# Attention with a learned metric and a small MLP on one core: setup and first block reordered, slots counted on

## The chip, the cores and the metric

One Trainium2 chip, one NeuronCore. The metric is the device time of one execution in microseconds, as the median of several runs. The engines are called TensorE (PE in the rows), VectorE (DVE), ScalarE (ACT), GpSimd (POOL) and SyncE (SP); SP's and POOL's queues issue the DMAs.

## The reference

The input x has 2048 tokens of 128 dimensions; there are 16 heads of 8 dimensions.

```python
h = layernorm(x) * (1 + ca) + sa
# attention
y = project(h)                                   # clip to +-8, y0 = sqrt(1 + sum(y^2) + eps)
v = d * dirv / (dn + eps)                        # log map: d = arccosh(y0), three square roots and a log
q, k, vv = v @ Wq.T, v @ Wk.T, v @ Wv.T
g = tanh(tanh((h - mu) @ W1.T + b1) @ W2.T + b2) * 0.1 + eta      # the metric, absolute value by sign
sc = (q * g) @ k.T / sqrt(8)                     # per head, 2048 x 2048
out = softmax(sc) @ vv
x = x + ga * project(mu0 + 0.1 * out @ Wo.T)
# MLP, 384 hidden, int weights scaled by 1/127
h = layernorm(x) * (1 + cb) + sb
x = x + gb * ((silu(h @ wg.T) * (h @ wu.T)) @ wd.T)
```

sa, ca, ga, sb, cb, gb are vectors from one small product.

## The kernel before

**Shapes.** Queries and keys are tiled in four blocks of 512 tokens (NB = 4), heads in four groups of four (NG = 4), keys in 16 tiles of 128. A query block is 64 steps: step j is head group j // 16 and key tile j % 16. In a step TensorE computes the scores of four heads in two halves (`score`, L703, 8 matmuls each, every one 32 columns wide, into one slot of two PSUM banks), ScalarE takes the exponential of each half (L510, 128x1024), and TensorE multiplies the exponentials of two steps earlier with the values (`product`, L720), accumulated over a head group in bank 6. VectorE evacuates bank 6 at each end of a head group (`evacuate`, L1100, `o_evac`); the first product of the next group waits for it.

**Slots.** There are three score slots, banks 0 to 5; half u of a block uses slot u % 3, so each block starts with slot 0, although 128 halves don't divide by 3. The exponentials lie in a ring of three steps, with an exception at the last step (`ring`). In steps 1 and 63 the product goes ahead of the first scores (`early`).

**Precision.** Queries and keys are split in three bf16 parts (hi, mid, lo), stored to DRAM and loaded back head by head with copies (SP's queue; POOL's queue for later blocks): `K_op`, `Q_op`. An extra row of the scores carries minus a bound on them: the square root of (largest key norm x query norm), per head and query. `nk` and `nq` are the norm products, `k_max` the reduction, `bound` the square root (ScalarE, L473), `shift` the scaled result (VectorE, L1013), which SP loads into `Q_op`.

**Setup.** Layer norm; transposes of h (L560) and copies (L420, `copy_hT`) for all blocks; the first metric product (`metric1`, L572); VectorE's chain for the log map with square roots and a logarithm from ScalarE (L435, L448); tanh of the metric; transposes of the values (`v_T`, `copy_vT`); keys (`k_of`, L609), the second metric product (`metric2`, L585), queries of block 0 (`q_of`). Keys of the blocks take turns in banks 2 and 3, the four norm products take turns in bank 0. Then a few idle matmuls (`keep_warm`, L674), the waits, and the loop. Each engine's queue runs in the order written.

**Work inside the loop.** In block 0 (`later`): value products (`v_of`, `V_AT`) behind steps 0, 1, 3 and 5, evacuated by VectorE (`values`, L1031); metric, queries and norms of blocks 1 to 3 at the steps of `M1_AT`, `M2_AT`, `Q_AT`, `NQ_AT`, all in bank 7 (`M_bank`); the three later roots by ScalarE behind step 49 (`ROOT_AT`). VectorE copies the norms out of bank 7 (`queries_norm`, L1065, gives `nq_sb`), and the next block's first metric product waits for that:

```python
if m == 0:
    pe.wait_ge(*((S["v_done"], NB) if b == 1 else (S["nq_sb"], b - 1)))
```

In blocks 1 to 3 the tail of the block before runs at the steps of `AT_...`: output projection, transposes, three gate and three up products (8 matmuls of 512 columns each) with a tanh each on ScalarE (L527), and four parts of the down product. All of them use bank 7. The last block's tail follows the loop. A second pass (p = 1) is there for scores beyond the bound; its branch is not taken here.

## Time and profile before

| | us |
|---|---|
| median of 3 runs | 607.02 (606.62 to 607.74) |
| profiled execution | 608.64 |
| span of its instructions | 606.6 |
| TensorE busy | 544.9 |
| ScalarE busy | 524.8 |
| VectorE busy | 152.6 |

Times in the rows are microseconds from the span's start, unless a column is said to be ns. A row of the timeline merges equal instructions that follow each other (x is how many), and what stands in brackets is the engine's idle time before it and what ended it. PEclk is the clock granted to TensorE, as a share of its full speed.

### The profile page before, as it was taken

To read this page: it belongs to the slowest core of one execution; us is meant where nothing else is said; L and a number is where in the kernel's file an instruction comes from. 1 tells how busy PE (TensorE), PEld (TensorE's weight loads), DVE (VectorE), ACT (ScalarE), POOL (GpSimd) and SP (SyncE) were. 2 spreads that over 40 slices of the span, in tenths; PEclk is the share of its full clock that TensorE was granted. 3 is DMA by queue.
4 is the path that set the end of the run, shared out by engine and by line. 5 is a ranking of instruction groups with operands and counts; after the bars stand their busy time and mean duration, and the time that the engine had idled before them with its cause. 6 is when DMAs were issued, how large, how long until landed. Compare 5 with 4: busy or idle time off the path is not lost.

```text
span 606.6 us, 16308 instructions
## 1 busy us (share of the span) xinstructions
PE 544.9 (90%) x7196; PEld 239.8 (40%) x7196; DVE 152.6 (25%) x420; ACT 524.8 (87%) x595; POOL 21.5 (4%) x25
## 2 busy tenths in 40 slices
PE   1466998999979999999999999999999999999544
PEld 0232543554423334455323444554334444543122
DVE  6963303030310361100003611000016211000363
ACT  3564898999999999999999999999999999999401
POOL 2300100000000010000000100000001000000010
PEclk9576999999989999999999999999999999999958
DMA  6012267010030200001002100000000000010000
GB/s 186 3 37 84 91 164 183 3 35 3 28 106 1 70 22 10 3 11 37 10 3 53 37 11 1 11 27 20 2 10 2 11 1 11 2 45 1 1 0 23
DMA packets 13626, 20.64 MB, mean 34 GB/s; under 512 B 2027, under 2 KB 10347, under 8 KB 13267
## 3 DMA queue, kind: packets, MB, share of 16 engines
q1 hardware_dynamic: 12707, 17.22, 11.0%
q0 software_dynamic: 560, 1.97, 0.9%
q8 instruction: 58, 0.95, 0.7%
q10 hardware_dynamic: 288, 0.40, 0.2%
q14 instruction: 13, 0.11, 0.1%
HBM read 13.15 MB, written 4.19 MB: 29 GB/s over the span
## 4 chain that ended last, share of the span: by engine, by line
PE 64%; ACT 15%; DVE 7%; issue 7%; DMA 4%; SPq 1%; POOL 0%; ACTq 0%; DVEq 0%
PE ps L703 27%; PE ps L720 26%; ACT probs L510 13%; PE ps L639 8%; DMA K_op<-k_scr 2%; DVE probs L939 1%; DMA k_scr<-arena 1%; DMA probs<-x_dram 1%; PE ps L674 1%; PE ps L609 1%; DVE arena L1143 1%; ACT arena L440 1%; SPq L262 0%; DVE kmax L1008 0%; PE ps L735 0%
## 5 line engine op out<-in xcount | busy, mean ns | idle before, releaser
L510 ACT ACTIVATE probs<-ps 128x1024 f32<-128x1024 f32 x512 | 481.4, 1116 | 16.9 <-PE ps L703 15.3
L703 PE MATMUL ps<-Q_op,K_op 73*32 73x512 bf16 x4096 | 293.0, 381 | 10.7 <-ACT probs L510 6.7
L720 PE MATMUL ps<-probs,V_op 128*32 128x512 f32 x2048 | 273.1, 595 | 1.2 <-ACT probs L510 0.8
L703 PEld LDWEIGHTS ps<-Q_op,K_op 73*32 73x32 bf16 x4096 | 122.5, 96 | 232.7 <-issue 120.5
L720 PEld LDWEIGHTS ps<-probs,V_op 128*32 128x32 f32 x2048 | 71.3, 110 | 49.3 <-issue 5.4
L1100 DVE COPY O_sb<-ps 128x512 f32<-128x512 f32 x16 | 11.1, 692 | 154.4 <-PE ps L720 154.4
L560 PE MATMUL ps<-fixed_sb,arena 128*128 128x128 f32 x32 | 7.4, 391 | 15.1 <-POOL arena L384 11.1
L1203 DVE SCALAR_TENSOR_TENSOR arena<-arena,ps 128x512 f32<-128x512 f32 x12 | 8.3, 688 | 45.0 <-ACT arena L527 45.0
L522 ACT ACTIVATE arena<-ps 128x512 f32<-128x512 f32 x4 | 2.8, 705 | 18.5 <-PE ps L735 18.5
L1209 DVE TENSOR_TENSOR arena<-ps,arena 128x512 f32<-128x512 f32 x12 | 8.3, 692 | 40.4 <-PE ps L639 40.3
L378 POOL TENSOR_TENSOR small<-small,half 128x4 f32<-128x4 f32 x4 | 4.1, 1014 | 404.6 <-DVE small L1173 404.6
L1221 DVE TENSOR_TENSOR arena<-ps,mod 128x512 f32<-128x512 f32 x3 | 2.1, 692 | 59.9 <-PE ps L639 59.9
L985 DVE TENSOR_SCALAR arena<-arena,cols 128x512 f32<-128x512 f32 x4 | 1.9, 485 | 60.2 <-ACT arena L431 60.2
L639 PE MATMUL ps<-w_att_sb,arena 128*32 128x128 f32 x256 | 10.2, 309 | 5.7 <-DVE arena L1147 5.7
L674 PE MATMUL ps<-ones_bf 128*128 128x512 bf16 x16 | 7.3, 627 | 7.9 <-POOL small L378 7.9
L1143 DVE RECIPROCAL arena<-arena 128x512 f32<-128x512 f32 x4 | 13.4, 3352 | 0.1
L639 PE MATMUL ps<-wd_f,arena 128*32 128x128 f32 x384 | 13.2, 272 | 0.0
L639 PE MATMUL ps<-arena,wg_f 128*32 128x512 f32 x96 | 12.9, 601 | 0.0
L560 PEld LDWEIGHTS ps<-fixed_sb,arena 128*128 128x128 f32 x32 | 5.3, 198 | 18.9 <-issue 8.4
L639 PE MATMUL ps<-arena,wu_f 128*32 128x512 f32 x96 | 12.7, 592 | 0.0
L639 PE MATMUL ps<-Q_op,w_sb 128*32 128x512 f32 x96 | 12.5, 591 | 0.0
L639 PEld LDWEIGHTS ps<-wd_f,arena 128*32 128x32 f32 x384 | 11.6, 109 | 2.3 <-issue 0.6
(162 smaller groups left out, 241.6 us busy)
## 6 DMA issues: line engine op xcount, KB each, us to landing
...
```

The costliest lines, as they stand in the source:

```text
L440: act.activation(h_tm[:, t, :], x_tm[:, t, :], ACT.Identity, scale=rstd[:, t:t + 1], bias=nmr[:, t:t + 1]).then_inc(S["xn_done"], 1)
L510: act.activation(probs[:, 2 * ring(j) + half_, :], slot_bank(u % 3), ACT.Exp)\
L560: ins = pe.transpose(bank(b % 2)[:, P * t:P * (t + 1)], src[:, TPB * b + t, :], ident_sb)
L609: pe.matmul(bank(2 + b % 2), wk_sb, vT[:, b, :], start=True, stop=True).then_inc(S["k_ps"], 1)
L639: ins = pe.matmul(to[CW * c:CW * (c + 1), :], weights[:, CW * c:CW * (c + 1)], moving, start=start, stop=stop, tile_position=(0, CW * c))
L674: ins = pe.matmul(to, ones_bf[:, 0:P], ones_bf[:, 0:BT], start=True, stop=True)
L703: ins = pe.matmul(slot_bank(u % 3)[CW * c:CW * (c + 1), i, :], K_op[0:rows, kt // TPB, h, at_k:at_k + CW], Q_op[0:rows, at_q:at_q + BT], s ...
L720: ins = pe.matmul(O_bank[32 * i:32 * (i + 1), :], V_op[:, kt, VW * h:VW * h + 32], probs[:, 2 * ring(j) + i // 2, BT * (i % 2):BT * (i % 2 ...
L1100: dve.tensor_copy(O_sb[:, g, :], O_bank).then_inc(S["o_evac"], 1)
L1143: c.did(dve.reciprocal(rec_T, rec_T))
L1203: dve.scalar_tensor_tensor(gl[m], th[m], 1.0, gates, ALU.add, ALU.mult).then_inc(S["gated"], 1)
L1209: dve.tensor_tensor(hid[:, m, :], ups, gl[m], ALU.mult).then_inc(S["glu_done"], 1)
```

## The change

- All four value products and their evacuations stand ahead of the loop, in banks 1 and 7 by turns; the loop waits for the last of them.
- The first block's metric (both products, three tanh) stands beside the normalisation, ahead of the roots of the log map; ten idle matmuls follow it. ScalarE loads the table of the square root once more right behind the logarithm.
- Each key block has its own bank (2 to 5); the key norms go to four groups of 32 rows of bank 0, with one reduction over all and three short copies. The key splits of blocks 1 to 3 come later in VectorE's order.
- The square roots for the query blocks 1 to 3 are computed on VectorE: a first guess by a shift and an addition on the bits, then one step with a reciprocal. `nq_sb` comes with the last operation; `shift(b)` follows at once, ahead of `evacuate(0, 2)` for the last block.
- In the first pass slots and ring are numbered on over all blocks, and no step is an exception; ScalarE's loop over blocks is written out.
- The tail's places in blocks 1 to 3 are spread over steps 8 to 55, and VectorE's evacuations of groups 1 and 2 are moved ahead of the last gate and of the result.

```diff
-AT_WO, AT_TR, AT_GATE, AT_UP, AT_DOWN = 8, 15, (19, 24, 29), (22, 27, 32), (37, 39, 41, 43)
-V_AT = (0, 1, 3, 5)
-M1_AT, M2_AT, Q_AT, NQ_AT, ROOT_AT = ((7, 10), (21, 24), (35, 38)), (13, 27, 41), (16, 30, 44), (19, 33, 47), 49
+AT_WO, AT_TR, AT_GATE, AT_UP, AT_DOWN = 8, 15, (19, 27, 35), (23, 31, 39), (43, 47, 51, 55)
+M1_AT, M2_AT, Q_AT, NQ_AT = ((7, 10), (21, 24), (35, 38)), (13, 27, 41), (16, 30, 44), (19, 33, 47)
...
-shift_f = [O_sb[0:H, 0, :], O_sb[0:H, 3, :], x_res[0:H, :, :].rearrange("p a b -> p (a b)"),
-           h_tm[0:H, 0:TPB, :].rearrange("p a b -> p (a b)")]
+shift_f = [O_sb[0:H, 0, :]] + [O_sb[0:H, 3, :]] * (NB - 1)
+root_a = x_res[0:H, :, :].rearrange("p a b -> p (a b)")
+root_b = sp_tm[0:H, 0:TPB, :].rearrange("p a b -> p (a b)")
...
-def ring(j):
-    return j % RING if j < STEPS - 1 else 1
+def slot(Bk, p, u):
+    return (u + 2 * STEPS * Bk) % 3 if p == 0 else u % 3
+def early(p, j):
+    return p == 1 and j in (1, STEPS - 1)
+def ring(Bk, p, j):
+    if p == 0:
+        return (STEPS * Bk + j) % RING
+    return 1 if j == STEPS - 1 else j % RING
...
+    pool.memset(hs_bf[:, H:2 * H], 0.0).then_inc(S["zero_ready"], 1)
...
-    for b in range(NB):
-        copy_hT(b)
+    copy_hT(0)
+    for m in range(MH):
+        tanh1(0, m)
+    copy_hT(1)
+    tanh2(0)
+    copy_hT(2)
+    copy_hT(3)
     root(y0, a2, 2)
     root(rt, t2, 3)
     root(dn, inn, 4)
     act.wait_ge(S["ln_in"], 1)
     act.activation(ln_u, u, ACT.Ln).then_inc(S["ln_out"], 1)
+    act.wait_ge(S["const_ready"], 2)
+    act.activation(kmax[:, 7:8], half[:, 0:1], ACT.Sqrt)
...
-    def k_split1(b):
+    def k_square(b):
+        act.wait_ge(S["k_ps"], b + 1)
+        act.activation(sqks[b], bank(2 + b), ACT.Square).then_inc(S["k_sq"], 1)
+    def k_high(b):
         act.wait_ge(S["k_ps"], b + 1)
         if b == 3:
             act.wait_ge(k_st[0], 16 * PARTS)
-        act.activation(k_parts[b][:, 0, :], bank(2 + b % 2), ACT.Identity).then_inc(S["k_hi"], 1)
-        act.activation(sqks[b], bank(2 + b % 2), ACT.Square).then_inc(S["k_sq"], 1)
+        act.activation(k_parts[b][:, 0, :], bank(2 + b), ACT.Identity).then_inc(S["k_hi"], 1)
...
-    def bound(b):
-        act.activation(shift_f[b], bank(6)[0:H, :] if b == 0 else shift_f[b], ACT.Sqrt,
+    def bound():
+        act.wait_ge(S["nq_ps"], 1)
+        act.wait_ge(S["kmax_ready"], 1)
+        act.activation(shift_f[0], bank(6)[0:H, :], ACT.Sqrt,
                        scale=kmax[0:H, NB:NB + 1]).then_inc(S["bound"], 1)
...
-    for m in range(MH):
-        tanh1(0, m)
     copy_vT(0)
     copy_vT(1)
-    k_split1(0)
-    tanh2(0)
+    k_square(0)
+    k_high(0)
+    copy_vT(2)
+    k_square(1)
+    q_split1()
     act.wait_ge(S["k_res"], 1)
     act.activation(k_parts[0][:, 1, :], rks[0], ACT.Identity).then_inc(S["k_mid"], 1)
-    q_split1()
-    k_split1(1)
+    k_square(2)
     act.wait_ge(S["q_res"], 1)
     act.activation(q_parts[0][:, 1, :], rqs[0], ACT.Identity).then_inc(S["q_mid"], 1)
-    k_split1(2)
-    k_split1(3)
     act.activation(sqq[:, :], g_fm[:, 0, :], ACT.Square).then_inc(S["q_sq"], 1)
-    bound(0)
+    k_square(3)
+    k_high(1)
+    bound()
     act.activation(silu_c[:, 1:2], c_c, ACT.Exp).then_inc(S["exp_table"], 1)
+    k_high(2)
+    k_high(3)
...
-            if j == ROOT_AT:
-                bound(b)
-    def block_steps(Bk, tails):
+    def block_steps(Bk, tails, p):
-                act.activation(probs[:, 2 * ring(j) + half_, :], slot_bank(u % 3), ACT.Exp)\
+                act.activation(probs[:, 2 * ring(Bk, p, j) + half_, :], slot_bank(slot(Bk, p, u)), ACT.Exp)\
...
     def blocks(p):
-        block_steps(NB * p, False)
-        with act.Fori(NB * p + 1, NB * (p + 1)) as Bk:
-            block_steps(Bk, True)
+        block_steps(NB * p, False, p)
+        if p == 0:
+            for Bk in range(1, NB):
+                block_steps(Bk, True, p)
+        else:
+            with act.Fori(NB * p + 1, NB * (p + 1)) as Bk:
+                block_steps(Bk, True, p)
...
-    for b in range(NB):
-        metric_T(b)
+    metric_T(0)
     for m in range(MH):
         metric1(0, m)
+    metric_T(1)
+    metric2(0)
+    metric_T(2)
+    metric_T(3)
...
     def k_of(b):
-        pe.wait_ge(*((S["vT_sb"], b + 1) if b < 2 else (S["vT_late"], b - 1)))
+        pe.wait_ge(*((S["vT_sb"], b + 1) if b < 3 else (S["vT_late"], 1)))
+        pe.wait_ge(S["m1_sb"], MH)
+        pe.matmul(bank(2 + b), wk_sb, vT[:, b, :], start=True, stop=True).then_inc(S["k_ps"], 1)
+    def v_of(b):
         if b >= 2:
-            pe.wait_ge(S["k_sq"], b - 1)
-            pe.wait_ge(S["k_res"], b - 1)
+            pe.wait_ge(S["v_done"], b - 1)
         else:
-            pe.wait_ge(S["m1_sb"], MH)
-        pe.matmul(bank(2 + b % 2), wk_sb, vT[:, b, :], start=True, stop=True).then_inc(S["k_ps"], 1)
-    def v_of(b):
-        pe.wait_ge(*((S["v_done"], b) if b else (S["q_f"], 1)))
+            pe.wait_ge(*((S["q_f"], 1) if b else (S["vT_late"], 1)))
         for t in range(TPB):
-            ins = by_columns(M_bank[:, P * t:P * (t + 1)], vT[:, b, P * t:P * (t + 1)], wv_sb)
+            ins = by_columns((M_bank if b % 2 else bank(1))[:, P * t:P * (t + 1)],
+                             vT[:, b, P * t:P * (t + 1)], wv_sb)
         ins.then_inc(S["v_ps"], 1)
     def nk(b):
         pe.wait_ge(S["k_sq"], b + 1)
-        pe.wait_ge(*((S["nk_done"], b) if b else (S["vT_late"], 1)))
-        pe.matmul(bank(0)[0:H, :], hs_bf[:, :], sqks[b], start=True, stop=True).then_inc(S["nk_ps"], 1)
+        pe.wait_ge(S["vT_sb"], 3)
+        pe.matmul(bank(0)[2 * H * b:2 * H * (b + 1), :], hs_bf[:, :], sqks[b], start=True, stop=True,
+                  tile_position=(0, 2 * H * b)).then_inc(S["nk_ps"], 1)
...
+    keep_warm(10, bank(5))
     v_T(0)
     v_T(1)
     k_of(0)
-    metric2(0)
+    q_of(0)
     v_T(2)
+    k_of(1)
     v_T(3)
-    q_of(0)
-    for b in range(1, NB):
-        k_of(b)
+    k_of(2)
     pe.wait_ge(S["hs_ready"], 1)
+    pe.wait_ge(S["zero_ready"], 1)
+    nk(0)
+    k_of(3)
+    nk(1)
+    nk(2)
+    nq(0)
+    nk(3)
     for b in range(NB):
-        nk(b)
-    nq(0)
+        v_of(b)
-        if j in V_AT:
-            v_of(V_AT.index(j))
...
-        if u >= 3:
+        if u >= 3 or (p == 0 and not start):
             pe.wait_ge(S["exped"], Bk * 2 * STEPS + u - 2)
         elif u < 2 and not start:
             pe.wait_ge(S["exped"], Bk * 2 * STEPS + u - 1)
...
-            early = j in (1, STEPS - 1)
-            if not early:
+            if not early(p, j):
                 score(Bk, j, p, 0)
             if j >= 2:
-                product(Bk, j - 2)
+                product(Bk, p, j - 2)
             elif tails:
-                product(Bk - 1, STEPS + j - 2)
-            if early:
+                product(Bk - 1, p, STEPS + j - 2)
+            if early(p, j):
                 score(Bk, j, p, 0)
...
-    keep_warm(7, M_bank)
-    for done, n in (("vT_late", 2), ("k_sq", NB), ("k_res", NB), ("nk_done", NB), ("bound", 1)):
+    pe.wait_ge(S["v_done"], NB)
+    keep_warm(4, M_bank)
+    for done, n in (("vT_late", 1), ("k_sq", NB), ("k_hi", NB), ("k_res", NB), ("nk_done", 1), ("bound", 1)):
         pe.wait_ge(S[done], n)
     blocks(0)
...
     dve.tensor_scalar(a2, n2, 1.0, EPS, ALU.add, ALU.add).then_inc(S["root_in"], 1)
+    def metric(b):
+        vec.after()
+        dve.wait_ge(S["m2_sb"], b + 1)
+        vec.did(dve.tensor_scalar(g_fm[:, b, :], g_fm[:, b, :], 0.1 * DH ** -0.5, eta_s, ALU.mult, ALU.add))
+    metric(0)
     dve.wait_ge(S["root_out"], 2)
...
-    def k_max(b):
-        dve.wait_ge(S["nk_ps"], b + 1)
-        dve.tensor_reduce(kmax[0:H, b:b + 1], bank(0)[0:H, :], AX.X, ALU.max).then_inc(S["nk_done"], 1)
+    def k_max():
+        dve.wait_ge(S["nk_ps"], NB)
+        dve.tensor_reduce(kmax[:, 0:1], bank(0), AX.X, ALU.max).then_inc(S["nk_done"], 1)
+        dve.wait_ge(S["nk_done"], 1)
+        for b in range(1, NB):
+            vec.did(dve.tensor_copy(kmax[0:H, b:b + 1], kmax[2 * H * b:2 * H * b + H, 0:1]))
+        vec.after()
+        dve.tensor_reduce(kmax[0:H, NB:NB + 1], kmax[0:H, 0:NB], AX.X, ALU.max).then_inc(S["kmax_ready"], 1)
     def shift(b):
-        dve.wait_ge(S["bound"], b + 1)
+        dve.wait_ge(*((S["nq_sb"], b) if b else (S["bound"], 1)))
         dve.tensor_scalar(shift_bf[b], shift_f[b], -1.0 - 2.0 ** -7, HEADROOM, ALU.mult, ALU.add)\
             .then_inc(S["shift_ready"], 1)
     def k_rest(b):
-        dve.wait_ge(S["k_sq"], b + 1)
-        dve.tensor_tensor(rks[b], bank(2 + b % 2), k_parts[b][:, 0, :], ALU.subtract)\
+        dve.wait_ge(S["k_hi"], b + 1)
+        dve.tensor_tensor(rks[b], bank(2 + b), k_parts[b][:, 0, :], ALU.subtract)\
             .then_inc(S["k_res"], 1)
...
     def queries_norm(b):
         dve.wait_ge(S["nq_ps"], b + 1)
-        dve.tensor_copy(shift_f[b], M_bank[0:H, :]).then_inc(S["nq_sb"], 1)
+        vec.did(dve.tensor_scalar(root_a, M_bank[0:H, :], kmax[0:H, NB:NB + 1], None, ALU.mult))
+        vec.after()
+        vec.did(dve.tensor_scalar(root_b.bitcast(I32), root_a.bitcast(I32), 1, None,
+                                  ALU.logical_shift_right))
+        vec.after()
+        vec.did(dve.tensor_scalar(root_b.bitcast(I32), root_b.bitcast(I32), 0x1FBD0000, None,
+                                  ALU.add))
+        vec.after()
+        vec.did(dve.reciprocal(shift_f[b], root_b))
+        vec.after()
+        vec.did(dve.tensor_tensor(shift_f[b], shift_f[b], root_a, ALU.mult))
+        vec.after()
+        vec.did(dve.tensor_tensor(root_b, shift_f[b], root_b, ALU.add))
+        vec.after()
+        dve.tensor_scalar(shift_f[b], root_b, 0.5, None, ALU.mult).then_inc(S["nq_sb"], 1)
+    copy_vT(3)
+    queries(0)
     k_rest(0)
-    copy_vT(2)
-    copy_vT(3)
-    metric(0)
+    queries_rest(0)
     k_low(0)
-    queries(0)
-    queries_rest(0)
-    k_rest(1)
     queries_low(0)
-    k_rest(2)
-    k_max(0)
-    k_max(1)
-    k_rest(3)
-    k_max(2)
-    k_max(3)
-    dve.wait_ge(S["nk_done"], NB)
-    dve.tensor_reduce(kmax[0:H, NB:NB + 1], kmax[0:H, 0:NB], AX.X, ALU.max).then_inc(S["kmax_ready"], 1)
-    k_middle(1)
-    k_low(1)
-    shift(0)
+    k_max()
     dve.wait_ge(S["ones_ready"], 1)
     values(0)
+    shift(0)
     values(1)
+    k_rest(1)
+    k_middle(1)
+    values(2)
+    k_low(1)
+    values(3)
+    k_rest(2)
+    k_rest(3)
     k_middle(2)
     k_low(2)
-    values(2)
     k_middle(3)
     k_low(3)
-    values(3)
...
         queries_norm(b)
+        shift(b)
     evacuate(0, 2)
-    for b in range(1, NB):
-        shift(b)
...
             for m in range(NM):
+                if m == NM - 1:
+                    evacuate(Bk, 1)
                 tail.gated(m, M_bank)
                 tail.glu(m, M_bank)
-            evacuate(Bk, 1)
+            evacuate(Bk, 2)
             tail.result()
-            evacuate(Bk, 2)
```

## Rows read from the trace of the kernel before

**Rows 1.** The page: busy times, the chain that ended last.

```profile
PE 544.9 (90%) x7196; PEld 239.8 (40%) x7196; DVE 152.6 (25%) x420; ACT 524.8 (87%) x595; POOL 21.5 (4%) x25
...
PE 64%; ACT 15%; DVE 7%; issue 7%; DMA 4%; SPq 1%; POOL 0%; ACTq 0%; DVEq 0%
```

**Rows 2.** Timeline of ScalarE in the loop (start, duration, instruction, count, idle).

```profile
188.58 8.53 ACT L510 ACTIVATE probs<-ps 128x1024 f32<-128x1024 f32 x9
...
198.66 1.94 ACT L510 ACTIVATE probs<-ps 128x1024 f32<-128x1024 f32 x2 [0.27 <-PE ps L703]
...
233.87 0.85 ACT L527 ACTIVATE arena<-ps 128x512 f32<-128x512 f32 x1
234.34 9.74 ACT L510 ACTIVATE probs<-ps 128x1024 f32<-128x1024 f32 x10
...
283.78 36.77 ACT L510 ACTIVATE probs<-ps 128x1024 f32<-128x1024 f32 x40 [0.27 <-PE ps L703]
...
289.23 19.41 ACT L510 ACTIVATE probs<-ps 128x1024 f32<-128x1024 f32 x21
...
307.31 1.33 ACT L510 ACTIVATE probs<-ps 128x1024 f32<-128x1024 f32 x1
```

**Rows 3.** The chain that ended last, between 212 and 222 us (start, us, what).

```profile
213.90 0.86 PE ps L703 x16
...
220.81 0.86 PE ps L703 x16
```

**Rows 4.** Timeline of the setup.

```profile
25.84 2.94 PE L572 MATMUL ps<-Q_op,w_sb 128*128 128x512 f32 x4
...
27.26 0.21 ACT L435 ACTIVATE small<-small 128x16 f32<-128x16 f32 x1 [0.49 <-DVE small L944]
...
57.70 1.05 PE L703 MATMUL ps<-Q_op,K_op 73*32 73x512 bf16 x16 [2.24 <-DMA Q_op<-wmod_sb]
```

**Rows 5.** Three windows (busy us of each engine, then PEclk, DMA share, GB/s).

```profile
20.00:24.50 4.50, 1.46 (x6) 0.72 (x4) 4.43 (x13) 1.37 (x2) 2.25 (x2) 0.50 0.00 0
...
92.80:96.20 3.40, 2.08 (x28) 0.81 (x32) 0.46 (x1) 2.48 (x4) 0.00 (x0) 1.00 0.80 187
171.40:174.70 3.30, 3.29 (x24) 0.98 (x28) 0.00 (x0) 2.71 (x3) 0.00 (x0) 0.50 0.63 159
```

**Rows 6.** Timeline of the first block's steps 0 to 17.

```profile
58.36 1.94 ACT L510 ACTIVATE probs<-ps 128x1024 f32<-128x1024 f32 x2 [1.91 <-PE ps L703]
...
67.43 0.89 DVE L1031 COPY V_op<-ps 128x128 f32<-128x128 f32 x4 [2.38 <-PE ps L639]
...
76.48 1.02 ACT L510 ACTIVATE probs<-ps 128x1024 f32<-128x1024 f32 x1 [0.16 <-PE ps L703]
...
94.12 0.61 PE L703 MATMUL ps<-Q_op,K_op 73*32 73x512 bf16 x8 [1.74 <-DMA K_op<-k_scr]
```

**Rows 7.** Timeline around the later roots.

```profile
164.87 1.28 ACT L473 ACT_TABLE_LOAD   x1
...
170.49 0.61 PE L703 MATMUL ps<-Q_op,K_op 73*32 73x512 bf16 x8 [3.71 <-ACT probs L510]
```

**Rows 8.** Timeline around the query norms of the second and the fourth block.

```profile
102.71 0.68 DVE L1065 COPY O_sb<-ps 16x512 f32<-16x512 f32 x1 [1.33 <-PE ps L634]
...
105.78 1.21 PE L639 MATMUL ps<-Q_op,w_sb 128*32 128x512 f32 x8
...
160.08 0.68 DVE L1065 COPY arena<-ps 16x512 f32<-16x512 f32 x1 [1.52 <-PE ps L634]
...
163.99 1.07 PE L720 MATMUL ps<-probs,V_op 128*32 128x512 f32 x8
```

**Rows 9.** One row of the page, then two of the timeline: VectorE's operations.

```profile
L1143 DVE RECIPROCAL arena<-arena 128x512 f32<-128x512 f32 x4 | 13.4, 3352 | 0.1
...
99.50 0.69 DVE L997 TENSOR_TENSOR arena<-arena 128x512 f32<-128x512 f32 x1
...
168.48 0.34 DVE L1117 TENSOR_SCALAR wg_f<-wg_f 128x384 f32<-128x384 int32 x1
```

More of the change, by code:

```diff
@@ L107, in build @@
         place_num, place_den = fixed_sb[:, P + H:P + H + 32], fixed_sb[:, P + H + 32:P + H + 64]
-        hs_bf = sb("hs_bf", [P, H], BF16)
+        hs_bf = sb("hs_bf", [P, 2 * H], BF16)
         silu_c = sb("silu_c", [P, 2])
@@ L633, in nq @@
                 pe.wait_ge(S["q_f"], b + 1)
-                pe.matmul((M_bank if b else bank(6))[0:H, :], hs_bf[:, :], sqq[:, :], start=True, stop=True)\
+                pe.matmul((M_bank if b else bank(6))[0:H, :], hs_bf[:, 0:H], sqq[:, :], start=True, stop=True)\
                     .then_inc(S["nq_ps"], 1)
@@ L641, in by_columns, with keep_warm @@
                 return ins
+            def keep_warm(n, to):
+                for _ in range(n):
+                    ins = pe.matmul(to, ones_bf[:, 0:P], ones_bf[:, 0:BT], start=True, stop=True)
+                ins.then_inc(S["warm"], 1)
+            keep_warm(10, bank(5))
             v_T(0)
@@ L669, in later @@
                         nq(b)
-            def keep_warm(n, to):
-                for _ in range(n):
-                    ins = pe.matmul(to, ones_bf[:, 0:P], ones_bf[:, 0:BT], start=True, stop=True)
-                ins.then_inc(S["warm"], 1)
             def score(Bk, j, p, half_):
@@ L710, in score, with product @@
                 ins.then_inc(S["scores"], 1)
-            def product(Bk, j):
+            def product(Bk, p, j):
                 g, kt = divmod(j, NT)
@@ L801, in blocks @@
                         block_steps(Bk, True, p)
-                product(last, STEPS - 2)
-                product(last, STEPS - 1)
+                product(last, p, STEPS - 2)
+                product(last, p, STEPS - 1)
                 pe.wait_ge(S["o_evac"], NG * (last + 1))
@@ L882, in _ @@
             vec.did(dve.memset(flag_f[:, :], 1.0))
+            dve.wait_ge(S["c_in"], 16)
+            vec.did(dve.tensor_scalar(eta_s, eta_c, DH ** -0.5, None, ALU.mult))
             for b in range(NB):
@@ L979, in _ @@
                 ins.then_inc(S["v_ready"], 1)
-            def metric(b):
-                vec.after()
-                dve.wait_ge(S["m2_sb"], b + 1)
-                vec.did(dve.tensor_scalar(g_fm[:, b, :], g_fm[:, b, :], 0.1 * DH ** -0.5, eta_s, ALU.mult, ALU.add))
             def queries(b):
@@ L1032, in values @@
                         V_op[:, TPB * b + t, 0:H * VW].rearrange("p (h w) -> p h w", h=H)[:, :, 0:DH],
-                        M_bank[:, P * t:P * (t + 1)].rearrange("p (h i) -> p h i", h=H))
+                        (M_bank if b % 2 else bank(1))[:, P * t:P * (t + 1)].rearrange("p (h i) -> p h i", h=H))
                     if t < TPB - 1:
```

16 lines of the change are left out of this document (5 added, 11 removed).

## The prediction

> **What bounds the kernel now.** I read the page first: TensorE is busy 544.9 us and ScalarE 524.8 us of 606.6, and the chain that ended last runs mostly over TensorE, with ScalarE second [rows 1]. Two engines that close are a pipeline, so I went to the order of time. The reader is to see three stretches: the setup up to the first scores at 57.70 [rows 4], four query blocks of 64 steps, and the last block's tail. In the loop ScalarE sets a floor: 20 exponentials start between 289.23 and 307.31, 0.904 us apart, so a step (two of them) takes 1.808 us [rows 2]. TensorE without side work needs less: its step pieces start at 213.90 and, four steps later, at 220.81, so 1.727 [rows 3]. It recovers 0.081 us a step of whatever it lost. Everything above 1.808 per step is therefore either side work that TensorE can't recover, ScalarE work that is no exponential, or a wait. I priced the change as sums over this floor.
>
> **Setup.** Rows 4 hold its two ends: the square root that the logarithm of the values starts from is asked of ScalarE and served at 27.26, and the first scores start at 57.70. The new order puts the first metric ahead of that root on ScalarE's queue, in strict order: copy, two tanh, copy, tanh, two copies, then a table load. TensorE's first metric product starts when the first copy is done, near 20.0. Its four passes took 2.94 us with the clock rising half way [rows 4]; it showed 0.50 between 20 and 24.5 [rows 5], where I take 3.6, so 23.6, tanh to 24.3, second product 1.9 at the full clock to 26.4 (3.6 at the lower one, to 28.1), tanh to 27.1, transposes and two copies to 28.3, table load 1.28 [rows 7] to 29.6. The root is 2.4 us late, and the values with it; VectorE has its own metric step done by then, so that costs nothing. In exchange the tanh work no longer stands between the values and the keys, and the four key norms no longer take turns with four reductions in one bank. By adding the same operations in the new order I get: first key product done 38.7, first query 42.6, last key norm 46.7, one reduction and three short copies to 48.0, square root of the first bound (no table load ahead of it) 48.8. Then VectorE has four value evacuations of 0.89 [rows 6], the first shift of 0.41, and, among others, three key remainders of 0.69 [rows 9], and TensorE waits for the last value block and the last remainder: 55.5. The query load, three issues behind the split of the queries, and the shift behind it land at about 55.6. First scores 55.7 against 57.70; with the ramp of the first exponential **1.7 us won**. If the second metric product runs at the lower clock, nothing is won (28.1 for 26.4, and all behind it 1.7 later); if the loads or the remainders are a little quicker, 3. Bounds: +1.5 and -3.5.
>
> **Values out of the loop.** The first 16 exponentials start between 58.36 and 76.48: 18.12 us, where 16 x 0.904 is 14.46 [rows 2, 6]. The 3.66 over the floor are the four value products of 32 matmuls and the lower clock of the start. Afterwards 0.5 stays for the ramp: **3.1 won**. It is hidden before the loop behind VectorE's chain, which is in the 55.7 above already.
>
> **The key load.** At 94.12 TensorE waits 1.74 us for the load of the second head group [rows 6]. By adding its operations in the new order, VectorE has split the last key block some 8 us behind the first shift; before, the four value evacuations wait between the splits for products in the loop (one of them at 67.43 [rows 6]). So the stores on POOL's queue and the loads behind them on SP's queue leave some 10 us earlier. The wait goes: **1.7 won**.
>
> **The later roots.** Before, ScalarE does three of them with a table load on either side: the load starts at 164.87, where the next exponential was due (164.6), and the next exponential starts at 169.42, 4.8 us late. TensorE, 3.71 us without work [rows 7], then shows clock 0.50 in the next stretch [rows 5], and ScalarE waits another 0.9 to 1.0 for it. Taken away: **5.8 won**. The table load is 1.283 us with the square root right behind it. "ScalarE: Activation LUTs" of the Trainium skill, section What ACT_TABLE_LOAD costs, counts a drain with each switch, about 2.66 us in all; two switches would then be 5.3 and the stop about 7.4. The trace measured 4.8, so the sum stays with it.
>
> What VectorE does instead: seven operations on 16x512 in a chain, each waiting for the one before, and only the last gives the semaphore that the old copy gave. Multiply from PSUM 0.68 (like the copy that it replaces [rows 8]); shift and add on integers, 0.34 for 384 columns [rows 9], so 0.43 each; reciprocal 3.35 [rows 9] (it has 128 partitions there, but the copies on 16 and on 128 partitions cost the same 0.68 to 0.69, so it is the 512 columns that count); two two-input operations at 0.69 [rows 9]; a last multiply of 0.41; six gaps of 0.04. Sum 6.9 us, against 0.68.
>
> Who waits: the next block's first metric product reads the same bank, and asks for this semaphore. Before, the copy starts at 102.71 and the product is reached at 105.78, so 3.07 us are free [rows 8]; the chain ends at +6.9, so TensorE stops 3.85 us. The same for the third block, with 3.25 free: 3.65. TensorE's queue is in order, the next scores stand behind it, and ScalarE has only 0.2 us of scores in hand there. Loss 3.7 + 3.4.
> The third chain starts at 160.08 and has no product behind it, but VectorE's own queue has: the shift (0.41) and then the evacuation of the third head group (0.69), which the first product of the fourth group waits for. It ends at 160.08 + 6.9 + 0.04 + 0.41 + 0.04 + 0.69 = 168.2; the product was reached at about 163.6 and started at 163.99 [rows 8]. Behind it stands the second half of the scores of this step: the second exponential of it starts at 169.6 and not at 165.5. Loss 4.1. So the stop of ScalarE turns into three of TensorE: **11.2 lost**.
> The clock: a wait of 1.74 left it at 1.00 [rows 5, 6], one of 3.71 sent it to 0.50 [rows 5, 7]. The new ones are 3.85, 3.65 and 4.6. At 0.50 TensorE's step is near 3.45 us, and with nothing in hand the stretch loses up to 1.6; the old case lost 1.0. I take 1.1 for the third and 0.75 x 1.6 for each of the others, where the stop may fall less well: **3.5 lost**; bounds 0 and 5. "TensorE: Matmul & The Clock Gate" of the Trainium skill, section HAM oscillation, says the same against this change: waits between bursts of matmuls make each burst start at the low clock. Rows 7 and 5 agree for 3.71 us.
>
> **Slots counted on.** Between 188.58 and 198.66, over the block's end, ten exponentials take 10.08 us and not 9.04 [rows 2]: the slots start over at 0 and TensorE waits for one still being read. With running numbers this goes, 1.04 at each of three ends, 0.5 at the last: **3.6 won** (at least 2, if VectorE's evacuation is late next).
>
> **The later tail places.** Behind the first gate's tanh, 49 exponentials start between 234.34 and 283.78: 49.4 us, floor 44.3 and two tanh of 0.47 (233.87 to 234.34) [rows 2]: 4.2 over it, TensorE being the bound throughout. The work stays the same; spread over 12 more steps it can use 12 x 0.081 = 1.0 more of ScalarE's pace. I take 0.9 in each of three blocks: **2.7 won** (bounds 0 and 4). VectorE's two reordered evacuations lie 10 steps before what needs them. ScalarE's unrolled loop I cost at nothing: blocks 0 and 1 already show the same 0.904.
>
> **Sum.** -1.7 - 3.1 - 1.7 - 5.8 + 11.2 + 3.5 - 3.6 - 2.7 = -3.9. The span of 606.6 becomes 602.7; the profiled execution took 608.64 with it, the median of the runs is 607.02, 0.4 above the span, so I forecast **603.1**.
>
> **The rivals.** (a) The forecast, three stops with the lower clock behind them: 603.1; chance 0.5, own range 601 to 605.5. (b) The stops are there, the clock stays, and the setup wins 3: 603.1 - 3.5 - 1.3 = 598.3, to 601; 0.2. For it: the new stops may straddle two stretches; against it [rows 5, 7]. (c) The change's roots don't stop anybody, because the reciprocal is short on 16 partitions (the price of 16 columns, 0.25, is no guide): chain 4.2, free time 3.07, stops of 1.1, 0.9 and 1.4 in place of 11.2, no clock: 603.1 - 7.8 - 3.5 = 591.8; 0.05. (d) The other side: VectorE's chain is longer than its parts. Only the integer operations are shown with another shape and other ALU functions; each extra us counts three times, since every stop has no cover left. From 1.7 us more per chain (8.6 in all) the gain is gone; with both integer operations at the reciprocal's 3.35 it would be 5.8 more, 17 us, 620. A milder form, 2.4 more a chain: 610. Chance 0.15. (e) The setup is not won, the metric at the lower clock: 603.1 + 1.7 to 3.2 = 605 to 606.3; 0.1.
> Below 597.5 lies (c) and a little of (b), above 609 half of (d): range 597.5 to 609. A change of 0.2% is 1.2 us here, about what a measurement of this kernel tells from none. Faster (under 605.8): (a), (b), (c) and half of (e), 0.80 less 0.06 for the upper edge of (a): 0.74; same 0.11 (the rest of (e) and that edge); slower 0.15, which is (d).
>
> **What would show it.** Right: scores start near 55.7; TensorE waits of 3 to 4.6 us for the root chain's last operation at two metric products, and for an O_sb copy at the start of the fourth head group; clock 0.50 behind them; no table load inside the loop; no gaps of 0.27 at block ends. Wrong: a reciprocal of 16x512 far from 3.35, the root of the logarithm later than 31, first scores later than 58, or block ends that still wait.

## The result and the profile after

The changed kernel takes 610.15 us (median of 9 runs, 609.16 to 611.84), the kernel before 607.74 on the same chips (9 runs, 604.7 to 609.02): ratio 1.0043, 95% interval 1.0024 to 1.0061. It is slower, by 0.4%. The forecast was 603.1, faster, with a range of 597.5 to 609, and the result lies outside it. The profiled execution took 609.74 with a span of 607.9 (before: 608.64 and 606.6). Times and ratios are those of fast runs; of one kernel of the experiments (evac_first) two of ten runs, 971.57 and 2000.25 us, are left out by this.

The page of the changed kernel: busy times, chain, and the group of the exponentials (busy us, mean ns | idle before, releaser).

```profile
PE 545.7 (90%) x7203; PEld 240.7 (40%) x7203; DVE 167.8 (28%) x437; ACT 519.4 (85%) x593; POOL 21.6 (4%) x26
...
PE 83%; DVE 8%; ACT 4%; DMA 2%; issue 1%; SPq 1%; POOL 0%; DVEq 0%
...
L528 ACT ACTIVATE probs<-ps 128x1024 f32<-128x1024 f32 x512 | 478.6, 1123 | 30.9 <-PE ps L732 29.4
```

Beside [rows 1] TensorE's busy time is the same, ScalarE's is 5.4 less (no tables and roots in the loop), and the span is no shorter: the exponentials now stand idle for 30.9 us before they start. The chain holds 83% TensorE instead of 64%.

The start of the changed kernel, timeline of TensorE and ScalarE: metric, root, first scores, first exponentials.

```profile
19.95 3.78 PE L594 MATMUL ps<-Q_op,w_sb 128*128 128x512 f32 x4 [1.58 <-ACT Q_op L431]
...
24.51 2.35 PE L607 MATMUL ps<-Q_op,w_sb 128*128 128x512 f32 x4
...
30.06 0.22 ACT L446 ACTIVATE small<-small 128x16 f32<-128x16 f32 x1
...
56.34 4.46 PE L732 MATMUL ps<-Q_op,K_op 73*32 73x512 bf16 x40 [1.59 <-DMA Q_op<-wmod_sb]
...
57.42 4.69 ACT L528 ACTIVATE probs<-ps 128x1024 f32<-128x1024 f32 x5 [5.84 <-PE ps L732]
63.21 12.24 ACT L528 ACTIVATE probs<-ps 128x1024 f32<-128x1024 f32 x13 [1.09 <-PE ps L732]
```

The new order runs as it was added up: first metric product at 19.95 (forecast 20.0), root at 30.06 (29.6), first scores at 56.34 (55.7, and 57.70 in [rows 4]). The first exponential starts at 57.42 against 58.36 in [rows 6], 0.94 earlier, and 1.09 are lost again at 63.21.

The root chain of the second block, timeline of VectorE, TensorE and ScalarE in the changed kernel.

```profile
97.43 0.74 DVE L1102 TENSOR_SCALAR x_res<-ps,kmax 16x512 f32<-16x512 f32 x1 [1.33 <-PE ps L660]
98.21 0.42 DVE L1104 TENSOR_SCALAR arena<-x_res 16x512 int32<-16x512 int32 x1
98.66 0.41 DVE L1107 TENSOR_SCALAR arena<-arena 16x512 int32<-16x512 int32 x1
99.11 3.34 DVE L1110 RECIPROCAL O_sb<-arena 16x512 f32<-16x512 f32 x1
102.48 0.68 DVE L1112 TENSOR_TENSOR O_sb<-O_sb,x_res 16x512 f32<-16x512 f32 x1
103.19 0.68 DVE L1114 TENSOR_TENSOR arena<-O_sb,arena 16x512 f32<-16x512 f32 x1
103.91 0.41 DVE L1116 TENSOR_SCALAR O_sb<-arena 16x512 f32<-16x512 f32 x1
104.47 1.94 PE L665 MATMUL ps<-Q_op,w_sb 128*32 128x512 f32 x8 [3.62 <-DVE O_sb L1116]
...
107.30 1.02 ACT L528 ACTIVATE probs<-ps 128x1024 f32<-128x1024 f32 x1 [5.24 <-PE ps L732]
109.86 1.02 ACT L528 ACTIVATE probs<-ps 128x1024 f32<-128x1024 f32 x1 [1.54 <-PE ps L732]
```

The chain runs from 97.43 to 104.32, 6.89 us (forecast 6.9). Only the 0.74 at its head reads the bank; the product waits for the 0.41 at its end. The waits of TensorE in the first block of the changed kernel, 57 to 185 us (us in total, times, longest):

```profile
PE ps L665 <- DVE O_sb L1116: 7.2, 2, 3.6
PE ps L749 <- DVE O_sb L1144: 4.4, 2, 4.2
```

Three stops at the three places forecast, 3.62, 3.57 and 4.23 us (forecast 3.85, 3.65, 4.6). Windows of the changed kernel behind the first (two), the second and the third stop, columns as in [rows 5]:

```profile
103.90:107.20 3.30, 2.73 (x20) 1.04 (x24) 0.83 (x2) 0.00 (x0) 0.00 (x0) 0.50 0.00 0
107.30:110.50 3.20, 3.20 (x28) 1.09 (x24) 0.00 (x0) 1.66 (x2) 0.00 (x0) 0.50 0.00 0
141.40:144.70 3.30, 3.30 (x32) 1.37 (x27) 0.00 (x0) 1.66 (x2) 0.00 (x0) 0.50 0.00 0
175.50:178.80 3.30, 3.30 (x28) 1.53 (x24) 0.41 (x4) 1.05 (x2) 0.00 (x0) 0.50 0.36 99
```

The clock is at its lower level behind each stop, and behind the first for twice as long, 103.8 to 110.6 (6.83 us; 3.41 behind the others).

**Step lengths.** I take the time from the end of one step's second exponential to the end of the next step's; steps are numbered from 0 as in the kernel, and block 0 is taken to begin 1.83 us before the end of step 0. By ends the undisturbed loop takes 0.9165 us per exponential, 1.833 a step; the forecast measured starts, 0.904 and 1.808. In [rows 2] the difference is visible: the starts from 289.23 to 307.31 are 0.904 apart, but the last of them lasts 1.33 us, where one behind a pause lasts 1.02 [rows 6]; the durations grow by 12.5 ns from one to the next. In these records the starts run ahead of the ends, and a pause takes the lead back; so the pace of a long stretch is that of the ends. The four blocks of 64 steps:

| us | block 0 | blocks 1 to 3, each |
|---|---|---|
| before | 137.72 | 123.45 |
| after | 145.62 | 121.69, 121.68, 121.68 |

So 5.3 us are won in blocks 1 to 3 and 0.9 at the start, and block 0 has lost 7.9, in spite of the roots and the values that left it.

### The profile page after: what moved, and what is told of

The parts are those of the page before. It is cut to its first block, busy times and chain, and to the rows that moved or that the text cites. A ratio compares the mean times of both kernels' runs of the same rounds, so it can differ in the third digit from the quotient of the medians.

```text
span 607.9 us, 15940 instructions
## 1 busy us (share of the span) xinstructions
PE 545.7 (90%) x7203; PEld 240.7 (40%) x7203; DVE 167.8 (28%) x437; ACT 519.4 (85%) x593; POOL 21.6 (4%) x26
## 4 chain that ended last, share of the span: by engine, by line
PE 83%; DVE 8%; ACT 4%; DMA 2%; issue 1%; SPq 1%; POOL 0%; DVEq 0%
PE ps L732 36%; PE ps L749 35%; PE ps L665 8%; ACT probs L528 2%; DVE O_sb L1110 2%; ACT arena L451 1%; DMA probs<-x_dram 1%; PE ps L672 1%; PE ps L594 1%; PE ps L582 1%; DVE arena L1186 1%; DMA q_scr<-arena 1%; PE ps L575 0%; DVE O_sb L1144 0%; PE ps L764 0%
## 5 line engine op out<-in xcount | busy, mean ns | idle before, releaser
L528 ACT ACTIVATE probs<-ps 128x1024 f32<-128x1024 f32 x512 | 478.6, 1123 | 30.9 <-PE ps L732 29.4
L749 PE MATMUL ps<-probs,V_op 128*32 128x512 f32 x2048 | 274.3, 600 | 5.4 <-DVE O_sb L1144 4.4
L732 PEld LDWEIGHTS ps<-Q_op,K_op 73*32 73x32 bf16 x4096 | 124.7, 97 | 224.3 <-issue 131.0
L749 PEld LDWEIGHTS ps<-probs,V_op 128*32 128x32 f32 x2048 | 71.5, 112 | 54.1 <-issue 9.2
L665 PE MATMUL ps<-Q_op,w_sb 128*32 128x512 f32 x96 | 13.0, 631 | 7.2 <-DVE O_sb L1116 7.2
L665 PE MATMUL ps<-w_att_sb,arena 128*32 128x128 f32 x256 | 9.4, 292 | 6.4 <-DVE arena L1190 5.7
L665 PE MATMUL ps<-wd_f,arena 128*32 128x128 f32 x384 | 13.2, 272 | 0.0
L665 PE MATMUL ps<-arena,wg_f 128*32 128x512 f32 x96 | 12.7, 592 | 0.0
L665 PE MATMUL ps<-arena,wu_f 128*32 128x512 f32 x96 | 12.5, 592 | 0.0
L665 PEld LDWEIGHTS ps<-wd_f,arena 128*32 128x32 f32 x384 | 11.6, 109 | 2.2 <-issue 0.6
```

The costliest lines, as they stand in the source:

```text
L528: act.activation(probs[:, 2 * ring(Bk, p, j) + half_, :], slot_bank(slot(Bk, p, u)), ACT.Exp)\
L665: ins = pe.matmul(to[CW * c:CW * (c + 1), :], weights[:, CW * c:CW * (c + 1)], moving, start=start, stop=stop, tile_position=(0, CW * c))
L732: ins = pe.matmul(slot_bank(slot(Bk, p, u))[CW * c:CW * (c + 1), i, :], K_op[0:rows, kt // TPB, h, at_k:at_k + CW], Q_op[0:rows, at_q:at_q ...
L749: ins = pe.matmul(O_bank[32 * i:32 * (i + 1), :], V_op[:, kt, VW * h:VW * h + 32], probs[:, 2 * ring(Bk, p, j) + i // 2, BT * (i % 2):BT * ...
```

## The experiments

All are of the changed kernel unless said otherwise; ratios are to the kernel before, run on the same chip (606.75 us in experiments 1 to 4, 607.13 in 8 and 10, 606.95 in the others). A difference of two ratios from different experiments carries the noise of both.

**1. The bank given back by the operation that reads it (bank_early).** A semaphore of its own is given by the chain's first operation, and the next metric product waits for that.

```diff
-pe.wait_ge(... else (S["nq_sb"], b - 1))
+pe.wait_ge(... else (S["nq_rd"], b - 1))
-vec.did(dve.tensor_scalar(root_a, M_bank[0:H, :], ...)); vec.after()
+dve.tensor_scalar(root_a, M_bank[0:H, :], ...).then_inc(S["nq_rd"], 1)
+dve.wait_ge(S["nq_rd"], b)
```

> The changed kernel, but the bank is given back by the first operation of VectorE's root chain (its only read of PSUM), not by the last. Theory of the stops: the two waits of TensorE ahead of the metric products of the third and the fourth block (3.6 us each in the trace of the changed kernel, 6.8 and 5.4 us of the exponentials' time with the lower clock behind them) are gone, the third stop at the fourth head group stays; 610.2 - 12.2 = 598, below the kernel before. Rival, the chain's work itself or the reordered setup costs the time: the chains still run, so at most 3 us less, 607 to 610. Rival, only the wait counts and the low clock has another cause: 7.5 us less, 602.6.

599.81 us, ratio 0.989 (0.9855 to 0.9924), where the theory of the stops said 598. Stops one and two are gone; the third is left. Its row of the timeline, then two windows from the end of the wait on, columns as in [rows 5]:

```profile
162.76 1.93 PE L749 MATMUL ps<-probs,V_op 128*32 128x512 f32 x8 [4.23 <-DVE O_sb L1145]
...
161.80:165.10 3.30, 2.34 (x16) 0.82 (x20) 1.70 (x7) 0.00 (x0) 0.00 (x0) 0.50 0.31 89
165.20:168.50 3.30, 3.30 (x28) 1.24 (x24) 0.00 (x0) 1.94 (x2) 0.00 (x0) 0.50 0.15 27
```

The wait is the same 4.23 us, but the lower clock lasts 6.83 us here and 3.41 in the changed kernel, and steps 50 and 51 take 10.46 us in place of 9.30. That is 1.2 of the 1.8 us that are missing to 598.

**2. The evacuation ahead of the third chain (evac_first).** Only the third stop is addressed.

```diff
+                if b == 3:
+                    evacuate(0, 2)
                 queries_norm(b)
                 shift(b)
-            evacuate(0, 2)
```

> The changed kernel, but VectorE evacuates the third head group of the first block ahead of the last root chain. Theory of the stops: the third stop (4.2 us of TensorE, 5.6 us with the lower clock behind it) goes, the first two stay; 610.2 - 5.6 = 604.6. In its place the last shift comes 7 us later, which only loads a row for the next block, far ahead of its use. Rival, the later shift or the x load behind it delays the next block: no gain, 610.

603.8 us (forecast 604.6), ratio 0.9941 (0.9921 to 0.996). The waits on L665 stay at 7.2 in total, the one on L749 falls from 4.4 to 0.2.

**3. Both edits together (both).**

> Both edits. Theory of the stops: 610.2 - 17.8 = 592.4, and no wait of TensorE over 1 us inside the loop; the clock stays at 1.00 from the second step to the end of the loop. Rival of the chain's work: 604 to 607.

591.95 us (591.33 to 593.37), ratio 0.9752 (0.9719 to 0.9785). TensorE's waits in its first block, 57 to 185 us:

```profile
PE ps L732 <- DMA Q_op<-wmod_sb: 0.5, 1, 0.5
PE ps L749 <- DVE O_sb L1145: 0.2, 1, 0.2
```

All seven operations of each chain are still there, and the granted clock is 1.00 from 64.5 to 559.4. What the change lost are its stops: 610.15 - 591.95 = 18.2 us (17.7 by the two ratios). The same steps with and without their stop (lengths by ends):

| us | with | without (kernel) | cost | TensorE's wait |
|---|---|---|---|---|
| step 22 | 8.82 | 2.46 (bank_early) | 6.36 | 3.62 |
| step 25 | 2.27 | 1.83 (bank_early) | 0.44 | |
| step 36 | 7.41 | 2.37 (bank_early) | 5.04 | 3.57 |
| step 39 | 2.22 | 1.83 (bank_early) | 0.39 | |
| steps 50, 51 | 9.30 | 3.67 (both) | 5.63 | 4.23 |

Together 17.9, of which 11.4 are the waits. Steps 25 and 39 hold no stop. They follow the metric products behind steps 24 and 38, and in the kernels without the first two stops, and in experiment 4, they take 1.83; so their 0.44 and 0.39 belong to the stops and their clock, and the three stops cost 6.80, 5.43 and 5.63.

**4. The bank given back in the middle of the chain (bank_mid).** As in 1, but by the reciprocal, so that a wait of about half the size is left at the same two places: does a stop cost its wait, or its wait and the clock?

```diff
-vec.did(dve.reciprocal(shift_f[b], root_b)); vec.after()
+dve.reciprocal(shift_f[b], root_b).then_inc(S["nq_rd"], 1)
+dve.wait_ge(S["nq_rd"], b)
```

> As bank_early, but the bank is given back behind the reciprocal, 5.2 us into the chain and not 0.8 or 6.9. The two waits of TensorE shrink from 3.9 and 3.7 (counted from where it arrives) to 2.1 and 1.9. If the lower clock comes with any wait of this kind, each still costs 2 plus 1.5 to 2.9: 603.5 to 606. If a wait of 2 us leaves the clock at 1.00, like the 1.74 us wait of the kernel before, each costs 2 alone: 610.2 - 12.2 + 3.9 = 601.9. The trace says which, by PEclk behind the two waits.

603.46 us, ratio 0.9944 (0.9928 to 0.996). Its timeline at the two products, and after that ScalarE behind the first:

```profile
104.01 1.07 PE L665 MATMUL ps<-Q_op,w_sb 128*32 128x512 f32 x8 [1.74 <-DVE O_sb L1110]
...
134.61 1.07 PE L665 MATMUL ps<-Q_op,w_sb 128*32 128x512 f32 x8 [1.69 <-DVE O_sb L1110]
...
105.55 1.02 ACT L528 ACTIVATE probs<-ps 128x1024 f32<-128x1024 f32 x1 [2.07 <-PE ps L732]
106.85 1.02 ACT L528 ACTIVATE probs<-ps 128x1024 f32<-128x1024 f32 x1 [0.27 <-PE ps L732]
```

and the windows of the same kernel behind the two waits:

```profile
107.30:110.50 3.20, 3.20 (x45) 1.48 (x41) 0.00 (x0) 3.20 (x5) 0.00 (x0) 1.00 0.00 0
135.00:138.00 3.00, 3.00 (x44) 1.47 (x40) 1.69 (x4) 1.58 (x2) 0.00 (x0) 1.00 0.03 6
```

The clock stays at 1.00, where the same places after 3.62 and 3.57 us showed 0.50. At the first of the two places the eight products take 1.07 us instead of 1.94. Step 22 is 4.39, step 36 is 4.26, steps 25 and 39 are 1.83: the waits of 1.74 and 1.69 cost 1.93 and 1.89, which is the wait and 0.2. That splits the stops of the changed kernel, if the 0.2 holds for longer waits too: wait and 0.2 make 3.82, 3.77 and 4.43, 12.0 in all; the rest, 2.98, 1.66 and 1.20, goes with the lower clock, 5.8 in all.

The time of 603.46 is 1.6 above the 601.9 that was expected for a clock at 1.00, and at the edge of what was expected for the lower one; the clock and the step lengths decide here, not the time. The third stop, which this kernel still has, explains most of it: its wait is 4.24, the lower clock behind it again lasts 6.83 us (167.36 to 174.18), and its two steps take 10.58.

**5. The kernel before with the slots counted on (slots_only).** With them go the exceptions of `ring` and `early` in the first pass, and ScalarE's loop over blocks is written out; nothing else changes.

```diff
-act.activation(..., slot_bank(u % 3), ACT.Exp)
+act.activation(..., slot_bank((u + 2 * STEPS * Bk) % 3), ACT.Exp)   # and so in score, product, ring
```

> The kernel before with the slots and the ring numbered on alone (and ScalarE's loop written out, which they need). The prediction's term, read from the starts of the exponentials: 3.6 us less, 603 and a ratio of 0.994. Theory since: the starts run ahead of the ends, and by the ends steps 0 and 1 of a block lose only 0.76 us over 1.833 a step, at three block borders: 2.3 us less, ratio 0.996. Rival, the written-out loop of ScalarE costs something: no gain, ratio 1.000.

605.05 us, ratio 0.9969 (0.9948 to 0.9991), 1.9 us by the ratio. Each block border is 0.75 shorter (122.70 for 123.45), 2.3 in all, and not the 3.6 of the forecast. ScalarE's timeline in this kernel over the block border, where [rows 2] show a wait of 0.27 and here there is none:

```profile
174.24 26.70 ACT L520 ACTIVATE probs<-ps 128x1024 f32<-128x1024 f32 x29
```

**6. The kernel before with the tail's places and VectorE's order, nothing else (tails_only).**

```diff
-AT_GATE, AT_UP, AT_DOWN = (19, 24, 29), (22, 27, 32), (37, 39, 41, 43)
+AT_GATE, AT_UP, AT_DOWN = (19, 27, 35), (23, 31, 39), (43, 47, 51, 55)
```

> The kernel before with the later places of the tail and VectorE's reordered evacuations alone. The prediction's term: 2.7 us less. By the ends of the exponentials in the changed kernel it is 1.0 a block, 3.0 us less, ratio 0.995. Rival, the tail's spread brings nothing by itself and the changed kernel's 1.76 us per block are all the slots' doing: ratio 1.000.

604.78 us, ratio 0.9962 (0.9939 to 0.9985), 2.3 us by the ratio. A block takes 122.43 for 123.45: 1.02 each, 3.1 in three blocks (forecast 2.7). With experiment 5 this makes 1.77, the whole difference between 123.45 and 121.68.

**7. The later roots back on ScalarE (roots_back).** One copy of the norms on VectorE gives back the bank, as before the change; ScalarE does the three roots at step 49, and the shifts stand behind the evacuation again.

```diff
+if j == 49: bound(b)                          # ScalarE
-root chain of seven operations                # VectorE
+dve.tensor_copy(shift_f[b], M_bank[0:H, :]).then_inc(S["nq_sb"], 1)
```

> The changed kernel with the three later roots on ScalarE again, behind step 49, the bank given back by VectorE's copy, the shifts behind the evacuation. Theory of the stops: 17.8 us less for the three stops, 5.7 more for ScalarE's stop with the lower clock behind it: 610.2 - 12.1 = 598, ratio 0.984 to the kernel before. Rival, the later roots are not what made the change slow: 607 to 612.

599.06 us, ratio 0.9851 (0.9815 to 0.9887). Its timeline of ScalarE, and TensorE's wait:

```profile
160.85 1.28 ACT L495 ACT_TABLE_LOAD   x1
162.14 0.72 ACT L495 ACTIVATE O_sb<-O_sb,kmax 16x512 f32<-16x512 f32 x1
...
164.10 1.28 ACT L534 ACT_TABLE_LOAD   x1
165.40 4.69 ACT L534 ACTIVATE probs<-ps 128x1024 f32<-128x1024 f32 x5
...
166.47 0.62 PE L738 MATMUL ps<-Q_op,K_op 73*32 73x512 bf16 x8 [3.71 <-ACT probs L534]
```

The moved roots, with the order of semaphore and evacuation that came with them, are what made the change slower: without them it beats the kernel before by 1.5%. Done on VectorE without stopping anybody (experiment 3) they bring another 0.0099 of the time, 6.0 us, with an interval of about 3 to 9 (an estimate from the two intervals); the forecast said 5.8. By the step lengths the stop at the roots costs 5.7 in the kernel before (4.7 in step 50, 1.0 in step 52) and 7.2 in this one, because the lower clock behind it lasts 3.41 us there (from 171.3) and 6.83 here (from 167.2).

**8. The value products back in the loop (values_back).** In the kernel of experiment 3 they stand behind steps 0, 1, 3 and 5 again, with the seven idle products of before and nearly VectorE's order of before (the first shift now stands ahead of the key splits).

```diff
+V_AT = (0, 1, 3, 5)
+if j in V_AT: v_of(V_AT.index(j))             # in the loop
-for b in range(NB): v_of(b)                   # ahead of it
```

> The kernel both with the value products of the key blocks back in the first steps of the loop, where they stood before the change. By the term of the forecast they cost 3.1 there, and 1.7 more if the wait for the third key load comes back; by the step lengths of the changed kernel they cost 2.4 and the wait 1.9. So 594 to 596 against the 592 of both, a ratio of 0.979 to 0.982. The rival: with the stops gone the values lie in time that TensorE has to spare, and the time is that of both, 0.975.

595.81 us, ratio 0.9808 (0.9784 to 0.9833), so 0.0056 or 3.4 us above experiment 3, with an interval of about 1 to 6 (an estimate from the two intervals); by the ends of the last exponentials in the two traces it is 2.6. TensorE's waits in its first block, 57 to 185 us:

```profile
PE ps L730 <- DMA Q_op<-wmod_sb: 7.6, 1, 7.6
PE ps L730 <- DMA K_op<-k_scr: 0.8, 1, 0.8
```

The wait for the key load of the second head group comes back, at 0.8 and not at the 1.74 of [rows 6]. That wait isn't a fixed price: in the kernels of experiments 5 and 6, which leave the first block's keys and values as they were before the change, it was 0.4 (slots_only, first row) and 0.5 (tails_only) in the same list.

```profile
PE ps L717 <- DMA K_op<-k_scr: 0.4, 1, 0.4
...
PE ps L703 <- DMA K_op<-k_scr: 0.5, 1, 0.5
```

Step 16 took 1.83 us in both, and 2.97 in the profiled execution of the kernel before. The first scores are at 56.60, no earlier than the 56.34 of the changed kernel; TensorE only waits longer for the shift's row. So the values ahead of the loop lie in time that was idle, as the forecast had it.

**9. More idle products ahead of the loop (both_warm).** The kernel of experiment 3 loses most in steps 2 and 3 (3.22 and 2.18 us), with the clock at 0.50 from 54.3 to 64.5. TensorE waits several times between 49 and 57; idle products fill that.

```diff
+pe.wait_ge(S["bound"], 1)
+keep_warm(9, bank(6))
 pe.wait_ge(S["v_done"], NB)
-keep_warm(4, M_bank)
+keep_warm(8, M_bank)
```

> Both edits, and 17 idle matmuls in place of 4 in TensorE's last waits ahead of the loop (9 in bank 6 behind the last value product, 8 behind the last evacuation). If the lower clock at the start of the loop (0.50 from 54.3 to 64.5 in the run with both edits) comes from TensorE's 2.3 us wait ahead of it, the clock is 1.00 there, steps 2 and 3 lose their 1.7 us: 590.3 and a ratio near 0.972. If the idle matmuls end later than the load of the shift row, the first scores start later and it is as before or slower: 592 to 593.

591.23 us (589.9 to 591.76), ratio 0.9733 (0.9707 to 0.9759). The granted clock is 1.00 from 41.03 to the end of the loop and block 0 takes 126.42 instead of 128.35, but the loop starts 0.35 later, and the intervals of the two kernels overlap widely: a gain is seen in the trace and not shown by the times.

**10. The shift's row loaded ahead of the queries (shift_first).** In experiment 9 the first scores wait 1.21 us for that row, which stands last in SP's queue.

```diff
+sp.wait_ge(S["shift_ready"], 1)
+load_shift(0, 0, Q_first, 0)
 sp.wait_ge(q_st[0], 16 * PARTS)
 load_q(0, 0, Q_first, 0, GH)
-sp.wait_ge(S["shift_ready"], 1)
-load_shift(0, 0, Q_first, 0)
```

> The kernel both_warm with the queue's order at the first query block changed: the shift row's load is issued ahead of the load of the block's queries, instead of behind it. If the first score products wait last for the shift's row (they waited 1.21 us for it in both_warm), they come 0.6 to 1.2 us earlier than 57.45 and the time is about 590.5, a ratio of about 0.972 of the kernel before. The rival: the queries land just as late, since they then stand behind the shift's load in the queue; then the first scores stay at about 57.4 and the time is that of both_warm, a ratio of 0.973.

590.84 us (589.87 to 592.61), ratio 0.9735 (0.9709 to 0.9761). The first scores in its timeline:

```profile
56.26 1.48 PE L732 MATMUL ps<-Q_op,K_op 73*32 73x512 bf16 x24 [0.41 <-DMA Q_op<-q_scr]
```

They come 1.19 earlier and wait for the queries now; the loop ends 1.16 earlier (548.51 for 549.67). By the ratios it can't be told from experiment 9; the rival's 0.973 is as near to 0.9735 as the 0.972 expected, though its condition, scores at 57.4, didn't come. It is the best version by the trace, and 16 us under the kernel before.

## Why the prediction was wrong

**The step that failed.** The mechanism was right and the sizes were not; the largest miss is the step "The clock: ... 3.5 lost; bounds 0 and 5". It took one stretch of lower clock per stop, of one length; the runs showed stretches of 3.41 and of 6.83 us, and the lower clock behind the three stops cost 5.8 us, outside the step's own bounds. The gains fell short of their sum as well, by 2.9 us by the experiments, 3.8 by the medians.

**What held.** The mechanism did, step by step: the order of the setup, the root chain's 6.89 us (6.9), the three stops, their places and their releasers, and the 0.50 behind each. Experiments 1 to 3 show that the stops are all that stood between the change and a gain. Rivals (b), a clock that stays, and (c), a short chain, are out by the rows above. (e), the second metric product at the lower clock, is out too: it took 2.35 us, where the forecast put 1.9 for the full and 3.6 for the lower level. (d), a longer chain, gave the right sign for the wrong reason, since the chain was 6.89; by its own rule, three times each extra us against a gain of 3.9, it would have needed 1.3 more a chain and not 1.7. The sizes failed, on both sides of the sum:

| us | forecast | measured | by |
|---|---|---|---|
| start | -1.7 | -0.9 | first exponential 57.42 for 58.36 |
| values and key load | -4.8 | -3.4 | experiment 8, by the ratios |
| later roots removed | -5.8 | -6.0 | experiments 3, 7 |
| slots | -3.6 | -2.3 | experiment 5 |
| tails | -2.7 | -3.1 | experiment 6 |
| gains | -18.6 | -15.7; by the medians -14.8 | experiment 3: 606.75 to 591.95 |
| stops, waits | +11.2 | +12.0 | 3.8 + 3.8 + 4.4, experiment 4 |
| stops, lower clock | +3.5 | +5.8 | the rest of the step lengths |
| losses | +14.7 | +17.9 (12.02 and 5.84); by the medians +18.2 | 610.15 less experiment 3 |

The sum was a difference between two large numbers, -18.6 and +14.7. The gains were 3.8 too large and the losses 3.5 too small (by the medians), and each alone would have carried the forecast from 603.1 to about the time before; only both together make it slower. Of the single terms the clock's miss, 2.3, is the largest.

**The lower clock.** Step "The clock: ... 3.5 lost" took one low stretch per stop and at most 1.6 for it. For the third stop that was right (1.2, forecast 1.1), for the second nearly (1.7 for 1.2). Behind the first stop the clock stayed low for 6.83 us, twice the 3.41 of the others, and that cost 3.0 for 1.2. The length doesn't go with the length of the wait: the first two waits differ by 0.05 us, and the third stop, with 4.23 or 4.24 us, has 3.41 in the changed kernel and 6.83 in experiments 1 and 4, where it cost 2.4 and 2.5 instead of 1.2.

What TensorE did when the clock fell differs. It still waited, 0.7 to 1.0 us short of its next product, in four of the stops with 6.83 (the first one, also in experiment 2, and the third one in experiments 1 and 4). It had been working again for 0.3 to 1.4 us in those with 3.41. The stop at ScalarE's roots in experiment 7 is an exception, with 6.83 though it worked again for 0.7, so the runs show no rule; a forecast has to carry both lengths for each stop, which gives 3.6 to 9.0 us for three (1.2 or 3.0 each).

"TensorE: Matmul & The Clock Gate" of the Trainium skill, section HAM oscillation, has long waits between bursts of matmuls start each burst at the low clock. The runs agree roughly at 3.57 to 4.23 us, where the fall came up to 1.4 us into the burst; behind the short waits of 1.7 us, of which the section doesn't speak, the burst ran at the full one.

**The waits.** I took off what lies before the product (3.7 for 3.85) and nothing for the restart. Experiment 4 gives wait and 0.2.

**The slots.** "1.04 at each of three ends, 0.5 at the last" came from starts against 0.904. By ends a border costs 0.75, and three of them 2.3; a saving behind the fourth block no run isolates. The term was 1.3 too large, and it was a reading error; what shows it stands in [rows 2].

**Start, values, key load.** The first scores were 0.64 later than forecast, and the lower clock from 56.0 to 62.8 met them: step 2 took 3.04 for 1.83, where the forecast had left 0.5 for the whole ramp. By the step lengths of the two kernels the values were worth 2.4 for 3.1 and the key load 1.9 for 1.7. But 1.74 was one execution's wait, and a high one: it was 0.4 and 0.5 in experiments 5 and 6 with nothing changed ahead of it, and 0.8 in experiment 8. A price of one wait on a DMA, read from one trace, needs a bound of its own, and the sum gave it none.

**The roots.** The price from the trace, a stop of 4.8 and 1.0 for the clock behind it, gave 5.8, and 6.0 was measured by the ratios. By the drain that "ScalarE: Activation LUTs" of the Trainium skill counts with each switch, section What ACT_TABLE_LOAD costs, it would have been 8.4, an estimate (7.4 and 1.0). The interval of the times doesn't exclude that, the timeline of experiment 7 does: it has the root right behind the load again, and the two loads and three roots take 4.55 us (160.85 to 165.40).

**The chances.** 0.74 for faster rested on (a) having 601 to 605.5 as its own range, 4.5 us wide, around a sum of eight terms. The bounds that I had written down myself (clock 5 for 3.5, slots 2 for 3.6, nothing won at the start for 1.7) add 4.8 to it, 607.9, with no new mechanism at all. They were used for the edges of the range and not for the chance of the sign.
